# Low halves of the routed down weights on GpSimd instead of VectorE, their high halves earlier on ScalarE

## The reference

```python
scores = softmax(x @ gate_w.T);  top_w, top_i = top_k(scores, 6)
h  = silu(xb @ w1[e]) * (xb @ w3[e])      # xb: the tokens of expert e
ob = h @ w2[e]                            # w2[e]: 352 x 512, the down weights
y[token] += ob * top_w
out = x + y + (silu(x @ sw1) * (x @ sw3)) @ sw2
```

## Time and profile before

| what | value |
|---|---|
| median of three runs | 1001.88 us |
| span of the profiled execution | 1001.3 us |
| TensorE busy | 971.5 us (97%) |
| VectorE busy | 692.0 us (69%) |
| ScalarE busy | 593.1 us (59%) |
| GpSimd busy | 271.1 us (27%) |
| items with their end | from about 730 us to the end |
| low halves of w1, w3 (L1005) | 121.8 us in 76 instructions |

### The profile page before, as it was taken

How to read it: one execution, slowest core, us unless ns; L and a number is a source line. 1 busy time by engine, 2 the same in 40 slices (tenths; PEclk the granted TensorE clock), 3 DMA queues, 4 the chain that set the end, 5 groups by cost and what they waited for, 6 DMA issues and landing times.

```text
span 1001.3 us, 18374 instructions
## 1 busy us (share of the span) xinstructions
PE 971.5 (97%) x5548; PEld 838.0 (84%) x5549; DVE 692.0 (69%) x1053; ACT 593.1 (59%) x966; POOL 271.1 (27%) x170
## 2 busy tenths in 40 slices
PE   9999899999999999999999999989999999999996
PEld 7887798989898987788888888777888888888884
DVE  6655665676567675677876675656677888878886
ACT  6544665666666666445555552541267878778773
POOL 2200230323132142233333310010014545354541
PEclk9999999999999999999999999999999999999999
DMA  9100453321331332222212104410568989998995
GB/s 316 52 1 1 114 185 97 105 83 34 93 105 52 87 96 65 83 84 84 84 63 84 42 21 165 136 43 1 215 224 264 295 269 349 355 347 282 302 354 168
DMA packets 76144, 145.09 MB, mean 145 GB/s; under 512 B 13540, under 2 KB 41060, under 8 KB 75856
## 3 DMA queue, kind: packets, MB, share of 16 engines
q1 hardware_dynamic: 68256, 132.53, 39.2%
q0 software_dynamic: 7856, 12.16, 5.4%
HBM read 146.86 MB, written 15.07 MB: 162 GB/s over the span
## 4 chain that ended last, share of the span: by engine, by line
PE 72%; DMA 8%; SPq 6%; issue 5%; DVE 4%; ACT 4%; DVEq 0%; ACTq 0%; POOLq 0%
PE ps L327 19%; PE ps L328 18%; PE ps L329 18%; PE ps L712 6%; DMA w_and_lists<-in_w 4%; SPq L947 3%; PE ps L980 2%; PE ps L789 1%; DMA y_scratch<-ob,give 1%; PE ps L779 1%; PE ps L769 1%; SPq L1188 1%; DMA w_raw<-in_w 1%; DMA wo_raw<-in_owT 1%; PE ps L992 1%
## 5 line engine op out<-in xcount | busy, mean ns | idle before, releaser
L1005 DVE TENSOR_TENSOR w_l<-w_raw,w_h 128x1408 fp32r<-128x1408 f32 x76 | 121.8, 1624 | 30.9 <-ACT w_h L1001 18.7
L1001 ACT ACTIVATE w_h<-w_raw 128x1408 fp32r (+1 forms) x76 | 103.1, 1376 | 36.6 <-DMA w_raw<-in_w 29.2
L741 POOL TENSOR_TENSOR lw_l<-lw_raw,lw_h 128x1024 fp32r<-128x1024 f32 x32 | 77.1, 2414 | 144.7 <-ACT lw_h L737 139.3
L327 PE MATMUL ps<-w_h,xeT_h 128*128 128x352 f32 x288 | 97.5, 338 | 4.6 <-DVE w_l L1005 4.2
L328 PE MATMUL ps<-w_l,xeT_h 128*128 128x352 f32 x288 | 93.0, 323 | 0.0
L329 PE MATMUL ps<-w_h,xeT_l 128*128 128x352 f32 x288 | 92.9, 323 | 0.0
L1161 POOL DMA_INDIRECT xe<-xn_scratch,take x37 | 39.5, 1069 | 181.6 <-DVE give L1109 100.3
L1165 POOL DMA_INDIRECT y_scratch<-ob,give x34 | 79.7, 2345 | 22.6 <-issue 9.1
L327 PE MATMUL ps<-xT_hi,lw_h 128*128 128x512 f32 x192 | 77.3, 403 | 0.0
L328 PE MATMUL ps<-xT_lo,lw_h 128*128 128x512 f32 x192 | 76.5, 398 | 0.0
L329 PE MATMUL ps<-xT_hi,lw_l 128*128 128x512 f32 x192 | 75.5, 393 | 0.0
(11 more groups left out here) (327 smaller groups left out, 2741.9 us busy)
## 6 DMA issues: line engine op xcount, KB each, us to landing
w_raw<-in_w SPq DMA_DIRECT2D x78, 704.0 KB
w_and_lists<-in_w SPq DMA_DIRECT2D x39, 512.0 KB
w_and_lists<-in_w SPq DMA_DIRECT2D x39, 192.0 KB
rkB<-rk_scratch SPq DMA_DIRECT2D x56, 128.0 KB, 3.1
wq_raw<-in_Wq SPq DMA_DIRECT2D x8, 512.0 KB, 4.5
wo_raw<-in_Wo SPq DMA_DIRECT2D x16, 256.0 KB, 2.9
lw_raw<-in_kwT SPq DMA_DIRECT2D x8, 512.0 KB, 3.3
lw_raw<-in_qwT SPq DMA_DIRECT2D x8, 512.0 KB, 3.4
```

The source lines that it names most:

```text
L327: nc.tensor.matmul(out_ap, lh, rh, start=first, stop=False)
L741: e.tensor_tensor(lw_l[n][:, :, :], lw_raw[n][:, :, :], lw_h[n][:, :, :], ALU.subtract).then_inc(lw_ready[n], 1)
L1001: e.activation(w13_h[:, k, n, :, :], w13_raw[:, slot(raw), n, :, :], ACT.Copy).then_inc(w13_hi_s, 1)
L1005: e.tensor_tensor(w13_l[:, k, n, :, :], w13_raw[:, slot(raw), n, :, :], w13_h[:, k, n, :, :], ALU.subtract).then_inc(w13_ready, 1)
```

## The change

The low half of w2 (L1041 before) moves from VectorE, where it was an item's last instruction, to GpSimd, where it is the item's first, ahead of the gather and the scatter. The high half on ScalarE (L1037) moves from the end of the item to the place between `ob` and silu. GpSimd now also reads the raw slot's number of each item from the list (`raw_slot`), and VectorE reads it once less.

```diff
-        def ex_dve_w2(e, m, k, raw):
+        def ex_pool_w2(e, m, k, raw):
             e.wait_ge(w2_hi_s, m + 1)
             e.tensor_tensor(xT_lo[:, 2 * k:2 * k + 2, :], w2_raw[:, slot(raw), 0:FC - 1, :], xT_hi[:, 2 * k:2 * k + 2, :],
                             ALU.subtract).then_inc(w2_ready, 1)
...
                 ex_act_ob(e, i - 1 if ahead is None else ahead, k)
+            ex_act_w2(e, i, k, own)
             ex_act_silu(e, k, m + NSH)
             if not last and (not isinstance(m, int) or m > 0):
                 e.wait_ge(h3_ps, m + NSH)
                 ex_act_w13(e, 1 - k, 0, i + (k + 2), raw)
                 ex_act_w13(e, 1 - k, 1, i + (k + 2), raw)
-            ex_act_w2(e, i, k, own)
             return raw
...
             ex_dve_h(e, k, m + NSH)
-            raw = None if last else raw_slot(e, m + 1)
             if not last and (not isinstance(m, int) or m > 0):
+                raw = raw_slot(e, m + 1)
                 ex_dve_w13(e, 1 - k, 0, m * 2 + 7, raw)
                 ex_dve_w13(e, 1 - k, 1, m * 2 + 8, raw)
-            ex_dve_w2(e, m, k, own)
-            return raw
...
         def ex_pool(e, i, k):

             m = i * 2 + k
+            ex_pool_w2(e, m, k, 0 if isinstance(m, int) and m == 0 else raw_slot(e, m))
             e.wait_ge(xeT_ps, m + 2)
             e.wait_ge(take_ready, m + 4)
             e.sem_inc(acc_turn, 1)
             ex_gather(e, 1 - k)
...
             ahead_i = turn_ahead(e)
             for k in range(2):
+                ex_pool_w2(e, last_i * 2 + k, k, raw_slot(e, last_i * 2 + k))
                 ex_pool_scatter(e, ahead_i, k)
```

More of the change, by code:

```diff
@@ L1130, in ex_dve_ob_low, with ex_dve @@
                                    ALU.subtract).then_inc(home_ready, 1)
-        def ex_dve(e, i, k, own, ahead=None, last=False):
+        def ex_dve(e, i, k, ahead=None, last=False):
             m = i * 2 + k
@@ L1953, in _ @@
             ex_dve_w13(e, 1, 1, 8, raw_slot(e, 1))
-            raw = 0
             for m in range(4):
-                raw = ex_dve(e, m // 2, m % 2, raw)
+                ex_dve(e, m // 2, m % 2)
             with e.Fori(2, last_i) as i:
-                raw = ex_dve(e, i, 0, raw_slot(e, i * 2))
-                ex_dve(e, i, 1, raw)
+                ex_dve(e, i, 0)
+                ex_dve(e, i, 1)
             ahead_i = turn_ahead(e)
-            raw = ex_dve(e, last_i, 0, raw_slot(e, last_i * 2), ahead_i)
-            ex_dve(e, last_i, 1, raw, ahead_i, last=True)
+            ex_dve(e, last_i, 0, ahead_i)
+            ex_dve(e, last_i, 1, ahead_i, last=True)
             ex_dve_hT_low(e, last_i * 2 + 1, 1)
```

## The result

| | before | after |
|---|---|---|
| median of the runs shown with the result | 1001.94 us (4 runs, 999.18 to 1004.28) | 1018.91 us (4 runs, 1017.51 to 1020.85) |
| ratio to before, 95% interval | | 1.0162 [1.0136, 1.0187] |
| span of the profiled execution | 1001.3 us | 1016.0 us |
| TensorE busy | 971.5 us | 977.9 us |
| VectorE busy | 692.0 us | 660.6 us |

The change costs 17.0 us by the medians and 14.7 us between the two profiled executions. The forecast was 1011 us with a range of 1003 to 1018, so the direction was right and the size too small: the median lies 0.9 us above the range. GpSimd is busy 104 us more, not 87, and VectorE only 31 us less, not 44. Little of this difference is the moved subtraction; most is other work that became longer.

What follows compares the result with a forecast made beforehand. TensorE, almost never idle, was taken as the bound, with DMA-bound stretches and a slackless ob-scatter-landing loop. Loop 6.3, item 4 1.7 and end 1.8 us sum to 9.8 on the 1001.3 us span: 1011 us, range 1003 to 1018.

Steps and rivals of the forecast that it cites:

- The loop is what decides: ob, scatter, landing and next ob of the same parity: no slack before, grows to 14.98 us for two items.
- by the sum: Sign in the profile after: TensorE's idle time, not its busy time, grows by the summed 9.8 us.
- I count the gain at nothing: VectorE loses 36 subtractions, 43.8 us: no gain, at the most the 3.7 us of TensorE's idle time.
- The scatter 5.78 us behind ob: GpSimd's scatter starts 5.78 us after the start of ob instead of 4.72, behind high half, subtraction and gather.
- the ceiling of the end: At the program's end, 3.4 us lost if GpSimd must first wait out one of VectorE's w_l.
- From the start of a scatter to the buffer being free 9.2 us: Landing in the loop, taken as 9.2 us before ob of the same parity can start.
- first regime: Stretches where an item takes TensorE's own 6.91 us; forecast to slow to 7.49 an item, together 6.3 us.
- Still under the 7.66 of the stretch that the DMA bounds. So only the first regime slows: Loop at 7.49 us an item stays under the loads' 7.66, so the DMA-bound stretches lose nothing.
- ceiling of 10.0 us for the landing: Upper end of the loop term: with a 10.0 us landing, 7.89 us an item and 11 us lost.
- The rival that it gets worse: In 15 DMA-bound items GpSimd's subtraction holds up VectorE's take, give and w_l: 9 us more, 1020; chance 0.14.
- Item 4: ob waits for the first scatter there; w_l starts 4.13 us behind ob instead of 2.45, costing TensorE 1.7 us.
- The end: Last scatter stands behind item 35's w2 subtraction, 4.43 us after ob: 1.8 us lost.

Runs made afterwards that it cites:

- short landings: Changed kernel with scatters that overwrite instead of adding, sums of the routed experts left out: 1002.4 us; the same edit in the kernel before: 996.18 us.
- the control: Kernel before with VectorE's w_l made by a reduction that reads only w_h, low half of w1 and w3 left out: 1002.45 us, ratio 1.0000.
- the one-operand kernel: Changed kernel with VectorE's w_l made by a reduction that reads only w_h, low half of w1 and w3 left out: 1005.92 us, ratio 1.0041.

## Why the prediction was right and where it was wrong

- **The loop is what decides: right.** ob waits for scatters 18 times, as forecast "well above 5.8 us in total", and short landings take most of the loss away. TensorE's idle time was to grow "by the sum" and its busy time not at all; of the 14.7 us of the spans 6.4 are busy time.
- **"I count the gain at nothing": not contradicted.** VectorE's freed 43.8 us brought nothing that any run shows, though none has this alone; with the hold-ups gone and its work taken off, the time is still 3.5 us over the control.
- **The scatter 5.78 us behind ob: wrong; this is where the failure starts.** The sum of that step had "1.05 for the gather". Started right behind the subtraction the gather runs into the w_l that the same subtraction had held back, and took 2.26 us (median). Those 1.2 us are the whole distance from 5.78 to 6.92. I had the two halves of it in the rows: w_l starts where the subtraction ends (4.13 us in both), and the scatter beside w_l took 2.50, but 1.63 where none ran. In the loop I read the hold-up of the earlier trace rows in one direction, GpSimd holding VectorE. The other direction stood only in the ceiling of the end, and for the subtraction, not for the DMAs.
- **"From the start of a scatter to the buffer being free 9.2 us": wrong as a constant.** In the first regime of the changed kernel it is shorter. The scatter of result 4 started at 783.05, and ob of result 6, at 789.84, did not wait:

```profile
783.05 1.77 POOL L1164 DMA_INDIRECT y_scratch<-ob,give  x1 [0.30 <-issue]
...
789.84 0.68 ACT L1051 ACTIVATE ob<-ps,wl 128x512 f32<-128x512 f32 x1
```

That is 6.8 us or less; other places between 764 and 835 us show 7.5 to 8.7, and the saturated stretch 9.2 to 10.2. Some 0.7 us of the difference is the scatter instruction itself, 1.77 us here and 2.50 in the earlier trace rows. This goes with a first regime that cost 3.3 us instead of the forecast 6.3, in spite of the later scatter.
- **"Still under the 7.66 of the stretch that the DMA bounds. So only the first regime slows": wrong, and the step that failed.** 6.9 to 7.1 us to the scatter and 9.2 to 10.2 for the landing make up to 16.84 us for two items, over the 15.32 of the loads. The two saturated stretches cost 7.4 us, forecast at nothing. The 7.49 us an item stood 0.17 under the bound, on a landing measured elsewhere and a gather measured without its new neighbour; so thin a margin needed a term. The forecast's own ceiling of 10.0 us for the landing gave 7.89 us an item, over 7.66, and still had no price for the saturated stretches. The rival that it gets worse had the right place and a near price (9 us), but it expected VectorE to be late there, and it was the scatter.
- **Item 4: right.** TensorE starts at 766.25 instead of 764.82: 1.4 us, forecast 1.7. Timeline of the changed kernel, answering to the earlier trace rows:

```profile
760.50 0.69 ACT L1051 ACTIVATE ob<-ps,wl 128x512 f32<-128x512 f32 x1 [2.59 <-DMA y_scratch<-ob,give]
...
763.90 3.83 DVE L1005 TENSOR_TENSOR w_l<-w_raw,w_h 128x1408 fp32r<-128x1408 f32 x2 [0.85 <-ACT w_h L1001]
...
766.25 0.43 PE L327 MATMUL ps<-w_h,xeT_h 128*128 128x352 f32 x1 [1.94 <-DVE w_l L1005]
```

w_l begins 3.40 us behind ob instead of 2.45 and takes 3.83 us instead of 3.16, together 1.6 us; 0.2 came back because ob itself was earlier.
- **The end: right in the place of the scatter.** It starts 4.33 us behind ob (993.87, 998.20), forecast 4.43. The chain then shows it with 7.07 us against 4.89; after that some is given back, and the end costs 2.5 us instead of 1.8.

```profile
998.20 7.07 DMA y_scratch<-ob,give
```

- **What is left.** The spans account for 14.7 us, the medians for 17.0; the profiled execution is one of the two shorter of the four. How much of the 17 is the w_l held back (later TensorE), how much the gather held (later scatter) and how much its tokens being late for TensorE (7.0 us of waits) was not separated: the one-operand kernel removes all three (w_l at most 1.62 us, gather 1.05, 1.0 us of waits for tokens). Why the landing takes 6.8 us in one place and 10.2 in another was not tried; it goes loosely with the DMA share between the start of the scatter and the next ob: 0.49 to 1.00 where that took 6.8 us or less, 0.78 to 1.04 where it took 9.2 or more.

No version tried that does all the work beats the kernel before.

## What to carry to other kernels

When work goes from VectorE to GpSimd, ask for each of GpSimd's instructions, its indirect DMAs among them, which VectorE instruction it will now run beside, and price it from a row with that neighbour; the mean of the line belongs to the old order. Put a buffer's whole loop (write, issue, landing, next write) beside every bound of the stage, the saturated one too, with the landing taken in that stretch. A delay is free only while the loop is shorter than all of them, and a margin of 2% is none.

## What the runs showed of the hardware

- An indirect DMA on GpSimd waits for a VectorE instruction with two SBUF operands that is already running. Alone the gather takes 1.05 us and the scatter 1.55 to 1.63; beside w_l 2.26 and up to 2.90. In some 90 of them in both timelines the length was that of the lone one plus what was left of the running w_l, less 0.1 to 0.2 us; two gathers that began within 0.03 us of a w_l were not held. With one SBUF operand on VectorE they are not held (1.05 and 1.59). The Trainium skill, page "SBUF — State Buffer", section "SBUF: two separate sides", states the exclusion for a GpSimd operation that reads SBUF; by these rows the indirect DMAs belong to it in this direction.
- The other direction is not seen: in the kernel before w_l began at 30 places while a gather was running, and none of its 76 w_l took more than 1.63 us.
- Two w_l in a row leave a place where GpSimd's waiting subtraction goes in: the pair takes 5.4 us instead of 3.16 (scatter, then subtraction, ScalarE's old order).
- A GpSimd instruction that only writes (iota) held no w_l: in 10 places w_l began while a filler ran, with 0.2 to 0.8 us of it left, and none of the 76 took more than 1.63 us.
- An indirect scatter that adds was in, with the buffer free, after 6.8 us or less to 10.2 us in one kernel, more often long where the DMA was full (a share of 0.49 to 1.00 at the short ones, 0.78 to 1.04 at the long ones).
